# Macaron block on one core: result scatters closer behind their tiles, waits between the first dispatch's scatters, and a reordered last stage

## The reference

```
x = x + 0.5 * moe(layernorm(x))
x = x + attention(layernorm(x))          # 16 heads of 8, relative positions
x = x + 0.5 * moe(layernorm(x))

moe(x):  n      = layernorm(x) * gamma + beta
         g1, g2 = softmax(top2(softmax(n @ router.T)))      # 8 experts
         out    = g1 * expert_a(n) + g2 * expert_b(n) + shared(n)
         expert, shared:  (silu(n @ Wg.T) * (n @ Wu.T)) @ Wd.T
```

## Time and profile before

| | |
|---|---|
| median of 3 runs | 2273.97 us (2272.74 to 2279.67) |
| the profiled execution | 2267.75 us |
| its span | 2265.8 us |
| busy PE | 2055.6 us, 91% of the span |
| busy DVE | 1849.0 us, 82% |
| busy ACT | 1351.1 us, 60% |
| busy POOL | 1336.5 us, 59% |

### The profile page before, as it was taken

The page is one execution under the profiler, slowest core; times in us unless marked ns, Lnnn a source line. Parts: engine busy times, 40 slices in busy tenths (PEclk is TensorE's granted clock), DMA queues, the critical chain, the costliest instruction groups (busy, mean ns, idle before and its releaser), DMA issues. The chain is left out here.

```text
span 2265.8 us, 64247 instructions
## 1 busy us (share of the span) xinstructions
PE 2055.6 (91%) x22864; PEld 1244.0 (55%) x22865; DVE 1849.0 (82%) x3842; ACT 1351.1 (60%) x3301; POOL 1336.5 (59%) x1961
## 2 busy tenths in 40 slices
PE   7664988996799999999999999999999997889968
PEld 4443988893344444444444444444444447889965
DVE  6543755667699999999999999999999995666648
ACT  4332544556766766666677667667666655445545
POOL 3665155553355557757757667667577583465554
PEclk8666999999999999999999999999999999999989
DMA  5222242217801111210111011012102104232226
GB/s 158 75 67 84 64 151 88 73 50 232 209 13 34 34 26 19 45 34 13 43 34 45 11 38 49 4 39 48 34 12 44 40 24 156 60 89 74 68 63 185
DMA packets 161414, 149.02 MB, mean 66 GB/s; under 512 B 51602, under 2 KB 135698, under 8 KB 160594
## 3 DMA queue, kind: packets, MB, share of 16 engines
q1 hardware_dynamic: 141984, 109.36, 18.6%
q0 software_dynamic: 17280, 35.56, 4.8%
q10 hardware_dynamic: 1874, 0.51, 0.1%
HBM read 86.76 MB, written 62.55 MB: 66 GB/s over the span
## 5 line engine op out<-in xcount | busy, mean ns | idle before, releaser
L1521 PE MATMUL ps_scores<-c_relw,arena_stats 64*64 64x512 f32 x4096 | 956.5, 598 | 0.0
L1972 ACT ACTIVATE arena_probs<-ps_scores,neg_max 128x512 f32<-128x512 f32 x1024 | 697.0, 684 | 393.6 <-DVE neg_max L1857 389.7
L1857 DVE TENSOR_REDUCE neg_max<-ps_scores 128x1 f32<-128x512 f32 x1024 | 650.0, 662 | 26.9 <-PE ps_scores L1521 24.6
L1509 PE MATMUL ps_scores<-arena_rows,arena_stats 64*64 64x512 f32 x2048 | 483.6, 598 | 5.6 <-ACT arena_probs L1972 3.7
L1509 PE MATMUL ps_scores<-c_batch,arena_stats 64*64 64x512 f32 x2048 | 475.3, 596 | 4.7 <-POOL arena_stats L1449 2.6
L1521 PEld LDWEIGHTS ps_scores<-c_relw,arena_stats 64*64 64x64 f32 x4096 | 277.0, 132 | 247.3 <-issue 185.1
L1654 DVE STREAM_TRANSPOSE arena_weights<-arena_probs 128x1024 f32<-128x1024 f32 x256 | 313.5, 1224 | 1.8 <-ACT arena_probs L1972 1.8
L1654 DVE STREAM_TRANSPOSE arena_results<-arena_probs 128x1024 f32<-128x1024 f32 x256 | 313.2, 1224 | 0.0
L1447 POOL TENSOR_TENSOR arena_stats<-arena_rows,c_mask 128x128 f32<-128x128 f32 x256 | 121.9, 476 | 193.2 <-PE ps_scores L1521 191.6
L1447 POOL TENSOR_TENSOR arena_stats<-c_batch,c_mask 128x128 f32<-128x128 f32 x256 | 121.5, 475 | 193.5 <-PE ps_scores L1521 192.3
L1421 POOL DMA_INDIRECT expert_out<-arena_results,f2x_to x142 | 139.4, 982 | 120.8 <-PE ps_scores L1577 73.7
(11 more groups left out here) (323 smaller groups left out, 4225.9 us busy)
## 6 DMA issues: line engine op xcount, KB each, us to landing
qkv_record<-f1c_rec SPq DMA_DIRECT2D x16, 768.0 KB, 3.9
c_batch<-dispatched SPq DMA_DIRECT2D x71, 129.0 KB
arena_rows<-dispatched SPq DMA_DIRECT2D x71, 129.0 KB
c_batch<-qkv_record SPq DMA_DIRECT2D x32, 256.0 KB
arena_rows<-qkv_record SPq DMA_DIRECT2D x32, 256.0 KB
f2c_Y<-expert_out SPq DMA_DIRECT2D x28, 256.0 KB, 3.3
c_Os<-expert_out SPq DMA_DIRECT2D x20, 256.0 KB, 4.1
f1c_Y<-expert_out SPq DMA_DIRECT2D x16, 256.0 KB, 4.3
```

What stands on the lines that cost most here:

```text
L1509: m = nc.tensor.matmul(out, SK[n // 2 % NS][p, h, :, :].rearrange("p h a -> p (h a)"), KT[q][p, h, :], start=True, stop=False)
L1521: m = nc.tensor.matmul(out, SR[n // 2 % NS][p, h, :, :].rearrange("p h a -> p (h a)"), R[p, w0:w0 + L], start=False, stop=True)
L1857: reduce_max(nmx[U % NPAIR][:, n % 2:n % 2 + 1], psS[U % NPAIR][n % 2][:], AX, negate=True).then_inc(s_mx, 1)
L1972: nc.scalar.activation(Pr[s][:, n % 2, :], psS[s][n % 2][:], ACT.Exp, bias=nmx[s][:, n % 2:n % 2 + 1], accum_out=rs[:, G % 2, tt:tt + 1]). ...
```

## The change

Five parts, named here for the text below.

**A.** In the first dispatch POOL's two waits in the second half of a pair are replaced by seven, one before each two scatters, for points in the next pair's routing: transposes (2), logits (1), and the 2nd, 7th, 12th and 18th of DVE's 18 operations of choosing. The last pair has none.
**B.** The result scatters of the first tiles trail by 3 from the first tile on.
**C.** The 16 scatters of the last pair in the second tiles go to two of every three tiles (13 to 35).
**D.** POOL and SP no longer wait for the result scatters at the end of the attention block, and SP doesn't load steps 0 and 1 there; the finish's SP waits for the scatters and loads steps 0 to 4. The finish's small buffers stand in one block of memory.
**E.** In the finish the whole normalisation is ACT's. `hidden` has four buffers; DVE does `hidden(0..3)` first, and then, for each s, `gated(s)`, `shared(s - 1)`, `hidden(s + 3)`.

```diff
                     wait(pool, (s_nb, KB * (s + 1)), (s_sc[s % 4], SC * (s // 4)))
-                    if s % 2 == 1 and p + 1 < PAIRS:
-                        wait(pool, (s_tp, s + 2))
                     for j in range(JT):
+                        if p + 1 < PAIRS:
+                            at = JT * (s % 2) + j
+                            if at in (1, 2):
+                                wait(pool, (s_tp, 2 * p + 2 + at))
+                            elif at == 3:
+                                wait(pool, (s_lg, 2 * p + 4))
+                            elif at >= 4:
+                                wait(pool, (s_D, KD * (p + 1) + (2, 7, 12, KD)[at - 4]))
                         for k in range(TOPK):
                             t = JT * s + j
-                            if k == 0 and s % 2 == 1 and j == JT // 2 and p + 1 < PAIRS:
-                                wait(pool, (s_lg, s + 3))
                             pool.indirect_dma_start(xd, bass.IndirectOffsetOnAxis(idx[:, k, t:t + 1], 0),
...
-                q, y, lag = n % 4, n % YR, max(3, 15 - n // 4)
+                q, y = n % 4, n % YR
...
-                        pool.wait_ge(x_gu, min(ET, n + lag))
+                        pool.wait_ge(x_gu, min(ET, n + 3))
                     else:
-                        pool.wait_ge(s_tx, min(ET, n + lag + 2))
+                        pool.wait_ge(s_tx, min(ET, n + 5))
...
-            for q in range(4):
-                sp.wait_ge(s_st[q], 16 * NG2 * ((ET - q + 3) // 4))
-            yv = yd[0:TOPK * TOK, :].rearrange("(k n p) d -> p k n d", k=TOPK, p=P)
-            for s in range(2):
-                for k in range(TOPK):
-                    sp.dma_start(R2["Y"][s][k], yv[:, k, tokens(s), :]).then_inc(R2["s_ga"][s], 16)
...
-                        if 0 <= n - LATE < TOPK * JP:
-                            send(LASTP, n - LATE)
+                        at = n - LATE
+                        if at >= 0 and at % 3 < 2 and at // 3 * 2 + at % 3 < TOPK * JP:
+                            send(LASTP, at // 3 * 2 + at % 3)
...
-            for q in range(4):
-                pool.wait_ge(s_st[q], 16 * NG2 * ((ET - q + 3) // 4))
...
-            for s in range(2, 5):
+            for q in range(4):
+                sp.wait_ge(s_rows[q], 16 * ROWS * ((ET - q + 3) // 4))
+            for s in range(5):
                 wait(sp, (s_cb, JT * (s - 3)))
                 load(s)
...
-            def normalize(s):
-                t = JT * s + JA
-                wait(dve, (s_tp, s - 2))
-                nc.vector.tensor_scalar(xn[s % 3][:, JA, :], XR[:, t, :], rstd[:, t:t + 1], shift[:, t:t + 1], ALU.mult, ALU.add
-                                        ).then_inc(s_nv, 1)
...
-                wait(dve, (s_sg, s + 1), (s_gu, s + 1), (s_dn, s - 1))
-                nc.vector.tensor_tensor(h[s % 2][:], psU[s % 2][:], sg[s % 2][:], ALU.mult).then_inc(s_h, 1)
+                wait(dve, (s_sg, s + 1), (s_gu, s + 1), (s_dn, s + 1 - HB))
+                nc.vector.tensor_tensor(h[s % HB], psU[s % 2][:], sg[s % 2], ALU.mult).then_inc(s_h, 1)
...
-            for s in range(2):
-                normalize(s)
+            for s in range(HB):
+                hidden(s)
             for s in range(NB + 1):
-                if s + 2 < NB:
-                    normalize(s + 2)
                 if s < NB:
-                    hidden(s)
                     gated(s)
                 if s >= 1:
                     shared(s - 1)
+                    if s - 1 + HB < NB:
+                        hidden(s - 1 + HB)
...
-                for j in range(JA):
+                for j in range(JT):
```

More of the change, by code:

```diff
@@ L195, in build @@
             R = gates(K, c, "f2", None)
+            R["s_st"] = [c.enter_context(nc.semaphore(f"f2x_out{q}")) for q in range(4)]
             attention(K, "f2", R)
@@ L1255, in attention @@
         s_ld = [SX(f"in{q}") for q in range(4)]
-        s_st = [SX(f"out{q}") for q in range(4)]
+        s_st = R2["s_st"]
         s_tx, s_xf, s_hl, x_gu, x_sg, x_h, x_dn, s_y, s_wl, s_to = (
@@ L2040, in finish @@
     with ExitStack() as c:
+        early = sb(c, f"{tag}_early", [P, 11 * L])
+        homes = [early[:, q * L:(q + 1) * L] for q in range(11)]
+        xn = [home.rearrange("p (j d) -> p j d", j=JT) for home in homes[0:3]]
+        nT, sg, h = homes[3:5], homes[5:7], homes[7:11]
+        assert 11 * L * 4 <= 49152
         Y = R["Y"] + [[sb(c, f"{tag}_Y{q}{k}", [P, JT, D]) for k in range(TOPK)] for q in range(2, NB)]
-        xn = [sb(c, f"{tag}_xn{q}", [P, JT, D]) for q in range(3)]
-        nT, sg, h = ([sb(c, f"{tag}_{x}{q}", [P, L]) for q in range(2)] for x in ("nT", "sg", "h"))
         psT, psG, psU = ([ps(c, f"{tag}_ps{x}{q}", [P, L]) for q in range(2)] for x in ("T", "gate", "up"))
@@ L2046, in finish @@
         S = Sems(nc, c, tag)
-        s_ga = R["s_ga"]
+        s_ga, s_rows = R["s_ga"], R["s_st"]
         s_st = S("stored")
-        s_n, s_nv, s_tp, s_nT, s_gu, s_sg, s_h, s_dn, s_pa, s_cb, s_out = (
-            S(x) for x in ("normed", "normed_dve", "transp", "nT", "gateup", "silu", "hidden", "down", "second", "first", "shared"))
+        s_n, s_tp, s_nT, s_gu, s_sg, s_h, s_dn, s_pa, s_cb, s_out = (
+            S(x) for x in ("normed", "transp", "nT", "gateup", "silu", "hidden", "down", "second", "first", "shared"))
         block = c.enter_context(nc.Block())
-        JA = JT - 1
+        HB, ROWS = 4, TR // P
         def tokens(s):
@@ L2135, in _ @@
                     wait(act, (s_tp, s + 1), (s_gu, s - 1))
-                    nc.scalar.activation(nT[s % 2][:], psT[s % 2][:], ACT.Identity, bias=bet[:], scale=gam[:]).then_inc(s_nT, 1)
+                    nc.scalar.activation(nT[s % 2], psT[s % 2][:], ACT.Identity, bias=bet[:], scale=gam[:]).then_inc(s_nT, 1)
                 if s >= 1:
@@ L2139, in _ @@
                     wait(act, (s_gu, b + 1), (s_h, b - 1))
-                    nc.scalar.activation(sg[b % 2][:], psG[b % 2][:], ACT.Silu).then_inc(s_sg, 1)
+                    nc.scalar.activation(sg[b % 2], psG[b % 2][:], ACT.Silu).then_inc(s_sg, 1)
                 if s + 2 < NB:
@@ L2146, in transposes @@
             def transposes(s):
-                wait(pe, (s_n, JA * (s + 1)), (s_nv, s + 1), (s_nT, s - 1))
+                wait(pe, (s_n, JT * (s + 1)), (s_nT, s - 1))
                 for j in range(JT):
@@ L2157, in _ @@
                     wait(pe, (s_nT, s + 1), (s_sg, s - 1), (s_h, s - 1))
-                    nc.tensor.matmul(psG[s % 2][:], sgT[:], nT[s % 2][:], start=True, stop=True)
-                    nc.tensor.matmul(psU[s % 2][:], suT[:], nT[s % 2][:], start=True, stop=True).then_inc(s_gu, 1)
+                    nc.tensor.matmul(psG[s % 2][:], sgT[:], nT[s % 2], start=True, stop=True)
+                    nc.tensor.matmul(psU[s % 2][:], suT[:], nT[s % 2], start=True, stop=True).then_inc(s_gu, 1)
                 if s >= 1:
@@ L2163, in _ @@
                     for j in range(JT):
-                        m = nc.tensor.matmul(psY[b % 2][:, j, :], h[b % 2][:, j * P:(j + 1) * P], sdT[:], start=True, stop=True)
+                        m = nc.tensor.matmul(psY[b % 2][:, j, :], h[b % HB][:, j * P:(j + 1) * P], sdT[:], start=True, stop=True)
                     m.then_inc(s_dn, 1)
```

## The result

The changed kernel took 2300.35 us (median of 4 runs, 2297.00 to 2302.74), the kernel before 2273.35 beside it: a ratio of 1.0114, interval 1.0088 to 1.0140, 27 us slower. The forecast was 2297.

The account below looks back on a forecast made before the run. Only stages where PE waits could gain: first dispatch, first tiles, second tiles with sends, and the finish. The sum -2 (A) - 24 (B) - 4 (C) - 1 (D) + 54 (E) = +23 on 2273.97 gave 2297 us, range 2268 to 2324.

Parts of the forecast that it names:

- The ring: Finish: PE's and DVE's queue orders put everything from shared(s-1) to shared(s) in series; 7.8 us per turn, 12 turns.
- Its own time at full clock: Finish: one turn without added costs takes 6.2 us, where a step took about 3.6.
- POOL's stretching: Finish: POOL's multiplications lengthen DVE's `gated`; 0.7 us per turn taken, from 0 to 1.44.
- The clock: Finish: PE idles over 3.1 us each turn and may then run at the low level; 0.9 us taken, 0 to 2.4.
- The start: Finish before the turns: `hidden(3)` at 18.4 us into the stage; with `gated` twice and `shared(0)`, 21.8.
- Rival 2: Finish: PE's clock stays low, 9.3 us per turn, +72 there, +41 in all, 2315 us; chance 0.22.
- rival 1: Finish: full clock and POOL idle, 6.2 us per turn, +35 there, +4 in all, 2278 us; chance 0.12.
- It is satisfied when POOL comes to it: First dispatch: POOL's new waits find their condition met, so cost nothing and free nobody; -2 us, near nothing.
- The 19.43 us stay: Last run of the first dispatch: the last pair has no waits, so DVE still stands still 19.43 us.
- if the free tile lets PE catch up: Second tiles: PE recovers in the one tile of three without sends; up to 12 of 16 us go, -4 taken.
- The other bound of the range: Second tiles: 2.67 scatters per tile, the density of the slow first tiles, cost 16.3 us over 24 tiles; no gain, 0.
- Rival 3: First dispatch: a wait frees the other engines, pairs take 20.2 us instead of 24.2, -28; in all -14, 2260 us; chance 0.11.

Follow-up runs that it names:

- the run above: Changed kernel with three idle 512-column products on PE after each gate_up(s) from s=4 in the finish: 2178.88 us, ratio 1.0219 to the kernel before.
- A undone: Changed kernel with DVE's old order in the finish, and POOL's two waits of before in the first dispatch: 2251.53 us, ratio 0.9893 to the kernel before.
- B undone: Changed kernel with DVE's old order in the finish, and the first tiles' scatter lag again falling from 15 to 3: 2265.88 us, ratio 0.9953.
- part E alone: Kernel before with only the finish's normalisation all on ACT, four buffers for h and DVE's new order: 2188.24 us, ratio 1.0258.
- pause: Changed kernel with DVE's old order in the finish, plus POOL waits in the last pair of the first dispatch: 2237.59 us, ratio 0.9859.

## Why the prediction was right

**E, +54 forecast, +54.5 measured.** The ring is where it was put, with the releasers that were named, and disappears from either of its two sides. Its own time at full clock was forecast at 6.2 us and is 6.44: DVE waits 4.10, then works 2.34. The two additions were sized wrongly in opposite ways. POOL's stretching was taken as 0.7 and is about 0.2 on the mean over 12 turns (four turns have `gated` at 1.5 to 1.9 instead of 1.13); with the clock held up it is 0.8, as the run above shows. The clock was taken as 0.9 and is 1.4: that is what DVE's waits in the 12 turns have beyond 4.10 (17.2 us), and what PE's bursts have beyond the 3.28 us of one at the high level. The turn is then 8.0 us, not 7.8. The start was over-estimated: `hidden(3)` began 16.0 us into the stage, not 18.4. Together 122.9 against 122.4, closer than the terms deserve: 3 us too little in the turns and 2.4 too much before them nearly cancel. Rival 2 (low clock in each turn, 9.3 us) describes three turns in 12, of 9.6; rival 1 (always high) three others, of 6.0 to 6.4. The Trainium skill ("TensorE: Matmul & The Clock Gate", HAM oscillation) tells of a kernel in which each stretch of work after a wait starts cold again. The trace agrees in kind, since eight of the 12 bursts began at the low level, but not each time anew: the burst at 2219.52 followed a gap of 3.15 and ran high. The length of the gap doesn't decide it here: 3.15 us went with low bursts and with high ones, and the burst at 2268.13, after 3.83, began high and fell on its way.

**B, -24 forecast, -22.6 measured**, and 23.2 when undone alone.

**A, -2 forecast, -3.4 between the two traces.** Near in size, but the size isn't shown to be A's (see A undone), and two steps failed. Up to the last destination row the kernel lost 1.6 us. "It is satisfied when POOL comes to it" held in most pairs, but in two of them POOL waited 3.11 and 2.48 us for DVE's 18th operation (line 526), and then 2.37 and 2.01 instead of about 4 before the next run; the pairs got no shorter by it (25.3 and 24.6 us). A row of POOL:

```profile
95.04 0.95 POOL L395 DMA_INDIRECT dispatched<-f1d_n,f1d_idx  x1 [3.11 <-DVE f_pdiff L526]
```

"The 19.43 us stay" failed in the changed kernel: PE and DVE got through to the first tile at 198 to 207 us and were held up afterwards for a shorter time, DVE for 8.64 us at most. But it came true with B undone (19.51), so A doesn't rule that stop out.

**C, -4 forecast.** The step that failed is "if the free tile lets PE catch up". The other bound of the range, no gain because the density of scatters is the same, was the right one: +2.9 in this pair of traces, within the variation.

**D, -1 forecast, -1.9 measured**: of the 10.8 us between the end of the last scatter and the finish, 8.8 stay.

Rival 3 (the first dispatch set free) has its answer too: in the changed kernel the pairs after the first took 24.3 to 25.3 us, against 21.3 to 26.1 before.

The sum was +23, the traces say +31.4 and the medians +27. What is left over between trace and forecast is C (7 us) and the 2 us of a stage that nobody changed. That the median nonetheless lies only 3 us from 2297 is partly luck: of the two medians the difference is 4 us less than of the two traces.

## What to carry to other kernels

When the order of one engine's queue is changed, follow one item through the queues of all engines that it passes: here two orders, neither of them costly alone, closed a ring in which PE and DVE took turns, and opening it on either side removed the loss. The four buffers of h didn't help, since the ring goes through the order of the queues. Where runs of POOL's indirect DMAs hold up the engines, count them per tile: here a backlog that was avoided at one place was paid for at another. And read each part from its own stretch, since the same code varied by 3 us and more from one program to the next. The best version of these is the changed kernel with DVE's old order in the finish: 0.9846 (0.9826 to 0.9866) and 0.9856 (0.9837 to 0.9875) of the time before on the one kind of chip, 0.9976 (0.9966 to 0.9985) on the other.

## What was not expected of the hardware

While POOL issues runs of indirect DMAs, the engines are held up on some chips only. The kernel before took 2273.35, 2274.72 and 2271.19 us in three groups of runs and 2131.71 and 2130.52 in two, 6% less, with the same instructions. The group of the last operation of a pair's destination rows (8 in all), on the first kind of chip in the kernel before and on the second in part E alone, whose dispatch is the same code:

```profile
L542 DVE CAST f1d_idx<-f1d_v x8: 170/171/171, 21.2 to 195.4; 128x8 uint32<-128x8 f32 x8
```
```profile
L542 DVE CAST f1d_idx<-f1d_v x8: 170/171/173, 21.2 to 123.8; 128x8 uint32<-128x8 f32 x8
```

One operation takes the same 171 ns, but all eight pairs are routed 72 us sooner. POOL issues its scatters at the same 1.26 us on both. The other differences lie in the same places: 21 us from the last row to the first copy (10.1 against 31.6), 23 in the first tiles (257.0 against 280.3), 22 in the second (270.1 against 291.7), together 138 of the 142 us. With attention (1384.4 and 1383.5 us) there is none. That is why the changed kernel with DVE's old order gains 33 us on the one kind and 5 on the other: what parts A and B avoid doesn't happen there. What makes the two kinds different no run here shows. The four groups of experiments ran on four different chips, so whether the chip itself makes the difference, or something else that changes between groups, isn't shown either.

Where the engines are held up, three places give about the same price. In the first tiles 24 scatters beyond two per tile went with 23 us, in the second tiles 16 sends with 15 us (143.3 against 128.3 on the other chip), and in pause 13 us came back with eleven scatters in a row. About 1 us for each scatter beyond what fits a tile is a regularity of these traces, not a tested law; the run with the thinner sends could have tested it, but fell on the other kind of chip.
